# Softmax probability as a difference of two exponentials, with ScalarE's and TensorE's queues in another order

## The chip, the cores and the metric

The kernel runs on one core of a Trainium2 chip. A core has TensorE (PE, matmuls; its weight loads are shown as PEld), VectorE (DVE), ScalarE (ACT), GpSimd (POOL) and SyncE (SP, which here issues the DMAs). Each engine works through its own queue in order; they are tied together by semaphores. The metric is device time in microseconds of one execution, the lower the better.

## The reference, cut to what matters

`x` is 8 x 56 x 56 tokens of 64 channels, float32. Two layers follow each other, each a mixer and a mixture of experts:

```python
# layer 0 mixer: 49 regions (8x8 tokens) per image, 8 heads of 8 channels
idx_r = top_k(q_region @ k_region, 4)                  # 4 regions for every region
attn  = einsum('..sd,..kd->..sk', qs * scale, key_g)   # 64 queries x 256 keys, per head
score, index = top_k(attn, 32)                         # the 32 largest scores of a row
a_g   = softmax(score)                                 # over those 32
out   = a_g @ v_sel                                    # then a depthwise 3x3 conv of v is added,
out   = out @ out_w + out_b                            # and the output projection
# layer 0 experts: 8 experts 64->64->64, top 2 by a softmax router, exact GELU
# layer 1 mixer: 3x3 convolution 64->64 with weights binarized to +-1
# layer 1 experts: 8 experts 64->128->64, top 2, exact GELU
```

The kernel doesn't gather the 32 selected values. It makes a probability for all 256 keys that is zero for those not selected, and multiplies it with all 256 values.

## The kernel before, in words

The work is cut into 392 regions of 64 tokens for the attention, and into 56 strips of 7 regions (448 tokens) for everything else. Four stages run in one software pipeline: `a` (normalise, q, k, v), `t` (choose the 4 regions), `b` (attention, one region at a time) and `c0`, `c1` (what is done with a strip in layer 0 and in layer 1: the mixer's end, the router, the experts). Time is written in **slots**: one slot is one region of stage `b`, 14 slots are one **turn** (two strips), and `b` takes 28 turns. The table `PLACES` says in which slot, and at which fraction of it, an engine's queue holds a step of another stage; a step repeats every 7 slots. So slots are alike modulo 7, and the text calls them slot 0 to slot 6 by that remainder. ACT's slots with experts (GELU) are: slot 0 with two experts of `c1`, slots 2 and 3 with two of `c0` each, slots 5 and 6 with three of `c1` each. Slot 1 holds the end of layer 0's mixer (`c0` step 0: the depthwise convolution and the output projection in one group of matmuls into `h_ps`, read by ACT as `c_yT`), slot 4 that of layer 1. Stage `a` has its matmuls and copies at the end of slots 0 and 1.

One region in stage `b`, before:

- PE multiplies q and k (`pe_scores`, L425) into `s_ps`, ACT copies them to `b_s` (`act_scores`, L435). This is done two regions ahead.
- DVE selects (`dve_select`): four rounds over four tiles of 128 x 256 scores; `MAX8` (L452) takes the eight largest of each row into `b_v8`, `MATCH_REPLACE8` (L463) writes the scores to `b_r` with those eight replaced by `GONE` (-3e38).
- ACT (`act_sum`, L475 and L478) negates the row maximum (`b_nm`), takes the exponential of the 32 selected scores with their sum (`b_den`), and then (`act_exp`, L485) the exponential of all 256 (`b_e`).
- POOL takes the reciprocal of the sum (L493, `b_rec`), makes a mask times that reciprocal from `b_r` (`pool_mask`, L502), and multiplies it into `b_e` (`pool_prob`, L510).
- PE transposes `b_e` in two halves (`pe_turn`, L524) into the one bank `pT_ps`, ACT copies each half (`act_turn`, L532, `b_pT`), PE multiplies with the values (`pe_values`, L545, `o_ps`), and ACT copies the result to `b_at` (`act_values`, L552). PE and ACT do these for region r-1 in slot r.

`b_s`, `b_r`, `b_e` have two buffers, so the selection of region r+2 waits until the probability of region r is done (`b_prob`). An expert is a matmul (L666), GELU on ACT (L737, `c_h`), a matmul that spreads its weight (L669) and its copy on ACT (L739, `c_cb`), a product on POOL (L762) and a matmul down (L685). GELU and Exp are in different tables of ACT, so a switch puts an `ACT_TABLE_LOAD` in its queue.

## Time and profile before

| | |
|---|---|
| time, median of 3 runs | 6430.86 us (6424.47 to 6435.86) |
| time of the profiled execution | 6440.11 us |
| its span, first to last instruction | 6438.2 us |
| busy: DVE, PE, POOL, ACT | 87%, 74%, 69%, 63% of the span |
| mean granted TensorE clock | 0.73 of full speed |

Busy shares are averages over a start (stage `a` alone), 28 turns with stage `b`, and an end in which only `c0` and `c1` run. An engine's idle time is put down in the profile to what released it. All times here are in us unless ns is written.

### The profile page before, as it was taken

Reading aid. Unit: us, or ns where it says so; the run is one execution under the profiler, and the core shown is the slowest. Engines: PE = TensorE matmul, PEld = TensorE weight load, DVE = VectorE, ACT = ScalarE, POOL = GpSimd, SP = SyncE. Lnnn points to the kernel's source line nnn. Section 1 sums busy time; section 2 is a strip of 40 time slices with the busy share of each in tenths; the row PEclk is TensorE's granted clock in tenths of the full one; section 3 lists DMA queues with packets and bytes.
Section 4 is the critical chain, followed back from the end, with each engine's and each line's share of the span. In section 5 each row is a group of like instructions: output and inputs, shape, how many; then the busy total and the mean of one; then the engine's idle time right before and its main releaser. Section 6 shows DMA issues by size and latency. Waiting matters only on the chain.

```text
span 6438.2 us, 135940 instructions
## 1 busy us (share of the span) xinstructions
PE 4737.3 (74%) x26938; PEld 2880.6 (45%) x26938; DVE 5596.4 (87%) x24453; ACT 4054.4 (63%) x10222; POOL 4425.8 (69%) x3986
## 2 busy tenths in 40 slices
PE   3566777777777777777777777777777777777776
PEld 1333444444444444444444444444444444444444
DVE  1999999988989998999989898989999899999941
ACT  2455666666666666666666666666666666666643
POOL 1667776767677776767677677767776777777742
PEclk9666767777777777777777777777777777777777
DMA  4111111111111111111111111111111111111100
GB/s 75 39 31 42 34 40 34 40 32 42 30 41 34 39 35 34 40 32 43 32 42 30 40 36 36 38 33 40 32 43 31 43 31 32 30 30 34 33 11 10
DMA packets 585501, 229.09 MB, mean 36 GB/s; under 512 B 481152, under 2 KB 580224, under 8 KB 584576
## 3 DMA queue, kind: packets, MB, share of 16 engines
q1 hardware_dynamic: 584576, 219.25, 15.4%
q8 instruction: 276, 4.52, 0.3%
q14 instruction: 649, 5.32, 0.3%
HBM read 150.14 MB, written 68.80 MB: 34 GB/s over the span
## 4 chain that ended last, share of the span: by engine, by line
PE 29%; ACT 18%; issue 16%; DVE 15%; POOL 12%; ACTq 0%; DVEq 0%; POOLq 0%; DMA 0%; SPq 0%
DVE b_v L452 7%; POOL b_r L502 5%; PE y_ps L685 4%; DVE b_r L463 4%; PE h_ps L611 4%; POOL c_h L762 4%; ACT b_x L478 3%; PE a_ps L666 3%; PE pT_ps L524 3%; PE o_ps L545 2%; ACT b_e L485 2%; ACT L737 2%; PE h_ps L666 2%; POOL b_rec L493 2%; ACT L478 2%
## 5 line engine op out<-in xcount | busy, mean ns | idle before, releaser
L463 DVE MATCH_REPLACE8 b_r<-b_v,b_r 128x256 f32<-128x256 f32 x4704 | 1879.1, 416 | 0.0
L502 POOL TENSOR_SCALAR b_r<-b_r,b_rec 128x256 f32<-128x256 f32 x1568 | 1777.1, 1147 | 119.6 <-POOL b_rec L493 119.6
L452 DVE MAX8 b_v<-b_r 128x8 f32<-128x256 f32 x4704 | 1649.2, 418 | 0.0
L524 PE MATMUL pT_ps<-k_ident,b_e 128*128 128x128 f32 x3136 | 669.9, 352 | 776.3 <-ACT b_pT L532 688.3
L493 POOL TENSOR_TENSOR b_rec<-b_den,k_mone 128x4 f32<-128x4 f32 x392 | 400.5, 1022 | 1153.5 <-ACT b_x L478 1150.2
L762 POOL TENSOR_TENSOR c_h<-c_h,c_cb 128x448 f32<-128x448 f32 x672 | 760.9, 1133 | 503.9 <-ACT c_cb L739 503.0
L524 PEld LDWEIGHTS pT_ps<-k_ident,b_e 128*128 128x128 f32 x3136 | 472.6, 180 | 1161.2 <-issue 1136.2
L510 POOL TENSOR_TENSOR b_e<-b_e,b_r 128x1024 f32<-128x1024 f32 x392 | 923.5, 2356 | 18.0 <-POOL b_r L502 14.4
L685 PE MATMUL y_ps<-k_w,c_h 128*112 128x64 f32 x5376 | 776.1, 298 | 181.1 <-POOL c_h L762 177.9
L685 PEld LDWEIGHTS y_ps<-k_w,c_h 128*112 128x112 f32 x5376 | 706.5, 210 | 404.1 <-issue 403.0
L452 DVE MAX8 b_v<-b_s 128x8 f32<-128x256 f32 x1568 | 551.1, 415 | 318.0 <-POOL b_e L510 201.2
L532 ACT ACTIVATE b_pT<-pT_ps 128x512 f32<-128x512 f32 x784 | 469.9, 599 | 432.3 <-PE pT_ps L524 432.0
L485 ACT ACTIVATE b_e<-b_s,b_nm 128x256 f32<-128x256 f32 x1568 | 662.1, 493 | 0.0
L463 DVE MATCH_REPLACE8 b_r<-b_v,b_s 128x256 f32<-128x256 f32 x1568 | 624.7, 413 | 0.0
L666 PE MATMUL h_ps<-c_xT,k_w 128*128 128x448 f32 x672 | 525.4, 879 | 74.0 <-issue 67.5
L425 PE MATMUL s_ps<-b_k,b_q 32*128 32x256 f32 x3136 | 559.5, 484 | 24.2 <-DMA b_q<-q_d 24.2
L435 ACT ACTIVATE b_s<-s_ps 128x512 f32<-128x512 f32 x784 | 427.0, 603 | 117.5 <-PE s_ps L425 117.3
L478 ACT ACTIVATE b_x<-b_v,b_nm 128x32 f32<-128x32 f32 x1568 | 484.2, 310 | 9.5
L666 PE MATMUL a_ps<-c_xT,k_w 128*128 128x448 f32 x672 | 451.5, 765 | 0.0
L425 PEld LDWEIGHTS s_ps<-b_k,b_q 32*128 32x128 f32 x3136 | 336.3, 233 | 155.7 <-issue 119.6
L463 DVE MATCH_VALUE_LOAD b_r<-b_v,b_r 128x8 f32 x4704 | 405.3, 86 | 0.0
L737 ACT ACTIVATE c_h<-h_ps,k_b 128x448 f32<-128x448 f32 x336 | 212.8, 633 | 271.2 <-PE h_ps L666 268.5
(146 smaller groups left out, 7904.9 us busy)
## 6 DMA issues: line engine op xcount, KB each, us to landing
q_d<-a_qe SPq DMA_DIRECT2D x56, 448.0 KB, 4.2
b_k<-k_d SPq DMA_DIRECT2D x1568, 16.0 KB, 2.0
b_v<-v_d SPq DMA_DIRECT2D x1568, 16.0 KB, 2.0
b_q<-q_d SPq DMA_DIRECT2D x392, 64.0 KB, 2.1
c_win<-vpad_d SPq DMA_DIRECT2D x56, 145.0 KB, 2.8
c_hm<-cpad_d SPq DMA_DIRECT2D x56, 145.0 KB, 2.3
vpad_d<-a_vT SPq DMA_DIRECT2D x56, 116.0 KB, 3.7
c_win<-vpad_d SPq DMA_DIRECT2D x56, 116.0 KB, 2.7
```

The source lines that it names most:

```text
L425: last = pe.matmul(s_ps[g][:, t * NKEY:(t + 1) * NKEY], b_q[r % RING][part, 2 * t:2 * t + 2, :].rearrange("c h t -> c (h t)"), b_k[r % RIN ...
L452: top = dve.max(out=b_v8[p][:, t, 8 * rnd:8 * rnd + 8], in_=src[:, t, :])
L463: last = dve.match_replace(out=b_r[p][:, t, :], in_to_replace=b_v8[p][:, t, 8 * rnd:8 * rnd + 8], in_values=src[:, t, :], imm_value=GONE)
L478: last = act.activation(b_x8[:, t, :], b_v8[p][:, t, :], ACT.Exp, bias=b_nm[p][:, t:t + 1], accum_out=b_den[p][:, t:t + 1])
L485: last = act.activation(b_e[p][:, t, :], b_s[p][:, t, :], ACT.Exp, bias=b_nm[p][:, t:t + 1])
L493: pool.tensor_tensor(out=b_rec[p][:, :], in0=b_den[p][:, :], in1=k["mone"][:, 0:HP], op=ALU.pow).then_inc(b_inv, 1)
L502: last = pool.tensor_scalar(out=b_r[p][:, t, :], in0=b_r[p][:, t, :], scalar1=GONE, scalar2=b_rec[p][:, t:t + 1], op0=ALU.is_le, op1=ALU.mult)
L510: pool.tensor_tensor(out=b_e[p][:, :, :], in0=b_e[p][:, :, :], in1=b_r[p][:, :, :], op=ALU.mult).then_inc(b_prob, 1)
L524: last = pe.transpose(pT_ps[:, col:col + 128], b_e[p][:, t, c * 128:(c + 1) * 128], k["ident"][:, :])
L666: pe.matmul(bank[:, 0:STRIP], w1[layer][:, g, :], D["xT"][:, :], start=True, stop=True).then_inc(S["h"], 1)
L685: last = pe.matmul(y_ps[0:TILE, t * C:(t + 1) * C], D["h"][g % 2][:, t * TILE:(t + 1) * TILE], w2[layer][:, g, :], start=False, stop=(g == ...
L762: pool.tensor_tensor(out=D["h"][g % 2][:, :], in0=D["h"][g % 2][:, :], in1=D["cb"][g % 2][:, :], op=ALU.mult).then_inc(S["hc"], 1)
```

## The change

The probability is now `(exp(s) - exp(r)) / sum`, where `s` are the scores and `r` the scores with the 32 selected replaced by `GONE`, so that exp(r) is zero there and equal to exp(s) elsewhere.

- ACT takes a second exponential, in place on `b_r`, in two halves (`act_rest`), each as soon as DVE has finished two of the four tiles.
- POOL subtracts (`pool_prob`, two halves); `pool_mask` is gone. The reciprocal is no longer multiplied in here: PE spreads it over the partitions with four small matmuls into the free columns of `o_ps`, ACT's copy to `b_at` is 256 columns wide instead of 128, and POOL multiplies the two halves of `b_at` once a strip (`NORM`, before the projection).
- The row maximum is taken after the first round, and exp(s) of region r+1 stands at the end of ACT's slot r. ACT's slot begins with the copy of the transposed half.
- PE's slot begins with the transposes and the scores too; steps that stood ahead of them now stand behind.
- `PLACES`: `c0` step 0 goes from 78.1 to 78.62 on PE and from 78.3 to 78.64 on ACT. Layer 1's normalisation, transpose and gate (`c1` steps 1 to 3 on DVE, 2 and GATE on PE and ACT) move a slot ahead.

```diff
 def dve_select(dve, tau, r):
-            dve.wait_ge(b_prob, reg + 1)
+            dve.wait_ge(b_prob, 2 * reg + 2)
+            dve.wait_ge(b_sum, reg + 1)
...
+        def act_exp(act, tau, r):
+            act.wait_ge(b_max, reg + 1)
             act.activation(b_nm[p][:, :], b_v8[p][:, :, 0], ACT.Copy, scale=-1.0).then_inc(b_neg, 1)
...
+        def act_rest(act, tau, r):
+            for half in range(2):
+                act.wait_ge(b_sel, 2 * reg + half + 1)
+                for t in range(2 * half, 2 * half + 2):
+                    last = act.activation(b_r[p][:, t, :], b_r[p][:, t, :], ACT.Exp, bias=b_nm[p][:, t:t + 1])
+                last.then_inc(b_rest, 1)
...
+        def pool_prob(pool, tau, r):
+            for half in range(2):
...
+                pool.wait_ge(b_rest, 2 * reg + half + 1)
+                pool.tensor_tensor(out=b_e[p][:, pair, :], in0=b_e[p][:, pair, :], in1=b_r[p][:, pair, :],
+                                   op=ALU.subtract).then_inc(b_prob, 1)
...
-        def pool_mask(pool, tau, r):
...
 def pe_values(pe, tau, r):
+            pe.wait_ge(b_inv, reg + 1)
+            for t in range(HP):
+                pe.matmul(o_ps[32 * t:32 * t + VH, 128:256], b_rec[r % 2][:, t:t + 1].broadcast_to([128, VH]), k["ident"][:, :],
+                          start=True, stop=True)
...
 def act_values(act, tau, r):
-                           o_ps[:, 0:128].rearrange("c (j h q) -> c j h q", j=2, h=RH), ACT.Copy).then_inc(b_att, 1)
+                           o_ps[:, 0:256].rearrange("c (j h q) -> c j h q", j=4, h=RH), ACT.Copy).then_inc(b_att, 1)
...
 def pe_c(pe, tau, i, step, layer, other):
-                    pe.wait_ge(b_att, NWIN * (s + 1) + 1)
+                    pe.wait_ge(b_nrm, s + 1)
...
 def pool_c(pool, tau, i, step, layer):
+            if step == NORM:
+                pool.wait_ge(b_att, NWIN * (s + 1) + 1)
+                pool.tensor_tensor(out=b_at[i][:, 0:2], in0=b_at[i][:, 0:2], in1=b_at[i][:, 2:4], op=ALU.mult).then_inc(b_nrm, 1)
...
-                ("c0", 0): 78.1, ("c0", TURN): 78.5, ("c0", TURNED): 78.68, ("c0", 2): 81.66, ("c0", GATE): 82.05,
+                ("c0", 0): 78.62, ("c0", TURN): 78.7, ("c0", TURNED): 78.8, ("c0", 2): 81.66, ("c0", GATE): 82.05,
...
 @block.scalar, slot r
-                            act_sum(act, b, r)
-                            act_exp(act, b, r)
-                        steps(act, "act", n, lo, r, fs, 0, 0.2)
                             act_turn(act, b, r - 1, 0)
+                        if on:
+                            act_rest(act, b, r)
                             act_scores(act, b, r + 2)
                             act_turn(act, b, r - 1, 1)
-                        steps(act, "act", n, lo, r, fs, 0.2, 0.4)
-                        steps(act, "act", n, lo, r, fs, 0.4, 0.6)
+                        if on:
+                            act_sum(act, b, r)
+                        steps(act, "act", n, lo, r, fs, 0, 0.2)
                             act_values(act, b, r - 1)
-                        steps(act, "act", n, lo, r, fs, 0.6, 1)
+                        steps(act, "act", n, lo, r, fs, 0.2, 1)
+                        if on and (r + 1 < SLOTS or not last):
+                            act_exp(act, b, r + 1)
```

On ACT a slot with two experts (slot 0) stands like this before; names in brackets are the semaphores waited for.

```order
L475 ACTIVATE b_nm<-b_v 128x4 [waits b_top,b_prob]
L478 ACTIVATE b_x,b_den<-b_v,b_nm 128x32 [waits b_neg]
...
L485 ACTIVATE b_e<-b_s,b_nm 128x256 x4
L737 ACT_TABLE_LOAD [waits c1_h]
L737 ACTIVATE c_h<-h_ps,k_b_1 128x448 [waits c1_used]
L739 ACTIVATE c_cb<-g_ps 128x448 [waits c1_h]
L532 ACTIVATE b_pT<-pT_ps 128x512 [waits b_pt,b_pv]
L435 ACTIVATE b_s<-s_ps 128x512 [waits b_qk,b_exp]
...
L532 ACTIVATE b_pT<-pT_ps 128x512 [waits b_pt]
L737 ACTIVATE c_h<-a_ps,k_b_1 128x448 [waits c1_h,c1_used]
```

And the same slot after, from its first instruction to `b_at`, with the region's second exponential in it:

```order
L536 ACTIVATE b_pT<-pT_ps 128x512 [waits b_pt,b_pv]
...
L488 ACTIVATE b_r<-b_r,b_nm 128x256 [waits b_sel]
...
L435 ACTIVATE b_s<-s_ps 128x512 [waits b_qk,b_exp]
L435 ACTIVATE b_s<-s_ps 128x512
L536 ACTIVATE b_pT<-pT_ps 128x512 [waits b_pt]
L495 ACTIVATE b_x,b_den<-b_v,b_nm 128x32 x4
...
L747 ACTIVATE c_h<-h_ps,k_b_1 128x448 [waits c1_h]
...
L749 ACTIVATE c_cb<-g_ps 128x448 [waits c1_h]
...
L561 ACTIVATE b_at<-o_ps 128x32x8 [waits b_pv]
```

The copies of the transposed halves have moved to the head of the slot; the exponentials and the sum stand between them and the first GELU, and exp(s) of the next region closes the slot.

On PE the group of `c0` step 0 (L611 to L616, later L621 to L626) in slot 1, before:

```order
L611 MATMUL h_ps<-c_win,lepe_tap 64x448 [waits c0_x_in0]
L611 MATMUL h_ps<-c_win,lepe_tap 64x448 x2
L611 MATMUL h_ps<-c_row,lepe_tap 64x448
L612 MATMUL h_ps<-c_cor,lepe_tap 64x448
L616 MATMUL h_ps<-b_at,k_att 64x448 [waits b_att]
L616 MATMUL h_ps<-b_at,k_att 64x448
L524 MATMUL pT_ps<-k_ident,b_e 128x128 [waits b_prob,b_ptc]
L524 MATMUL pT_ps<-k_ident,b_e 128x128 x3
L425 MATMUL s_ps<-b_k,b_q 128x256 [waits b_in3,b_sc]
```

and after, from the last of the slot's value matmuls on:

```order
L554 MATMUL o_ps<-b_pT,b_v 16x128 x3
L702 MATMUL g_ps<-ident_b,c_x 128x112 [waits c0_part]
L702 MATMUL g_ps<-ident_b,c_x 128x112 x3
L709 MATMUL g_ps<-ident_b,c_x 64x112 [waits c1_lc,c0_pT]
L709 MATMUL g_ps<-ident_b,c_x 64x112 x3
L621 MATMUL h_ps<-c_win,lepe_tap 64x448 [waits c0_x_in1]
L621 MATMUL h_ps<-c_win,lepe_tap 64x448 x2
L621 MATMUL h_ps<-c_row,lepe_tap 64x448
L622 MATMUL h_ps<-c_cor,lepe_tap 64x448
L626 MATMUL h_ps<-b_at,k_att 64x448 [waits b_nrm]
L626 MATMUL h_ps<-b_at,k_att 64x448
L640 MATMUL a_ps<-k_ident,c_yT 112x64 [waits c0_pT,c0_yT]
```

The group stood ahead of the slot's transposes and scores; it now stands behind everything of stage `b` in that slot, directly ahead of the transposes (L640) of its own result.

On POOL a slot of `c0`'s experts, before and after:

```order
L493 TENSOR_TENSOR b_rec<-b_den,k_mone 128x4 [waits b_sum]
L502 TENSOR_SCALAR b_r<-b_r,b_rec 128x256 [waits b_inv,b_sel]
L502 TENSOR_SCALAR b_r<-b_r,b_rec 128x256 x3
L762 TENSOR_TENSOR c_h<-c_h,c_cb 128x448 [waits c0_cb] x2
L510 TENSOR_TENSOR b_e<-b_e,b_r 128x1024 [waits b_exp,b_msk]
```

```order
L508 TENSOR_TENSOR b_e<-b_e,b_r 128x512 [waits b_exp,b_rest]
L508 TENSOR_TENSOR b_e<-b_e,b_r 128x512 [waits b_rest]
L516 TENSOR_TENSOR b_rec<-b_den,k_mone 128x4 [waits b_sum]
L775 TENSOR_TENSOR c_h<-c_h,c_cb 128x448 [waits c0_cb] x2
```

The probability no longer stands behind the reciprocal, the four masks and the experts' products.

## Rows read from the trace of the kernel before

**Rows 1.** The page: busy time by engine.

```profile
PE 4737.3 (74%) x26938; PEld 2880.6 (45%) x26938; DVE 5596.4 (87%) x24453; ACT 4054.4 (63%) x10222; POOL 4425.8 (69%) x3986
```

**Rows 2.** Timeline of DVE: first selections of turns 3, 23 and 27.

```profile
723.05 1.08 DVE L452 MAX8 b_v<-b_s 128x8 f32<-128x256 f32 x3 [0.22 <-issue]
5154.06 1.08 DVE L452 MAX8 b_v<-b_s 128x8 f32<-128x256 f32 x3
5965.81 1.41 DVE L452 MAX8 b_v<-b_s 128x8 f32<-128x256 f32 x4
```

**Rows 3.** Windows (busy of PE, PEld, DVE, ACT, POOL; clock; DMA): nine turns, late, end.

```profile
2719.70:4713.40 1993.70, 1503.21 (x8658) 915.70 (x8658) 1804.52 (x7848) 1313.11 (x3295) 1421.64 (x1280) 0.73 0.16 37
...
5000.00:6000.00 1000.00, 761.72 (x4517) 472.76 (x4517) 956.07 (x4187) 680.11 (x1724) 757.14 (x669) 0.75 0.14 33
6164.00:6438.20 274.20, 199.09 (x933) 120.68 (x931) 46.16 (x275) 97.23 (x174) 87.61 (x95) 0.74 0.05 12
```

**Rows 4.** DVE's waits in the nine turns: total, times, longest.

```profile
DVE b_v L452 <- POOL b_e L510: 89.9, 18, 5.8
DVE b_v L452 <- issue: 34.2, 27, 3.2
```

**Rows 5.** Timelines of POOL and DVE around one such wait.

```profile
2993.59 1.03 POOL L493 TENSOR_TENSOR b_rec<-b_den,k_mone 128x4 f32<-128x4 f32 x1 [11.16 <-ACT b_x L478]
2994.92 4.51 POOL L502 TENSOR_SCALAR b_r<-b_r,b_rec 128x256 f32<-128x256 f32 x4 [0.30 <-POOL b_rec L493]
3001.95 2.35 POOL L510 TENSOR_TENSOR b_e<-b_e,b_r 128x1024 f32<-128x1024 f32 x1
...
3004.43 1.41 DVE L452 MAX8 b_v<-b_s 128x8 f32<-128x256 f32 x4 [4.84 <-POOL b_e L510]
```

**Rows 6.** ACT's waits in the nine turns.

```profile
ACT b_pT L532 <- PE pT_ps L524: 140.2, 93, 5.3
ACT b_at L552 <- PE o_ps L545: 101.2, 108, 3.0
ACT b_nm L475 <- DVE b_v L452: 89.9, 18, 5.7
ACT c_h L737 <- PE h_ps L666: 84.1, 41, 3.5
ACT c_h L737 <- PE a_ps L666: 72.9, 64, 2.3
ACT b_s L435 <- PE s_ps L425: 35.5, 65, 1.4
ACT a_vT L351 <- PE a_ps L327: 32.7, 18, 1.9
ACT a_xT L337 <- PE a_ps L257: 28.3, 18, 2.1
```

**Rows 7.** Two groups of ACT in the nine turns.

```profile
L739 ACT ACTIVATE c_cb<-g_ps 128x448 f32<-128x448 f32 x216 | 116.2, 538 | 0.0
...
L552 ACT ACTIVATE b_at<-o_ps 128x128 f32<-128x128 f32 x126 | 34.9, 277 | 101.2 <-PE o_ps L545 101.2
```

**Rows 8.** Timelines of ACT and PE in slot 1.

```profile
2973.77 1.69 ACT L485 ACTIVATE b_e<-b_s,b_nm 128x256 f32<-128x256 f32 x4
2980.53 0.60 ACT L532 ACTIVATE b_pT<-pT_ps 128x512 f32<-128x512 f32 x1 [5.06 <-PE pT_ps L524]
...
2971.52 4.71 PE L611 MATMUL h_ps<-c_win,lepe_tap 128*64 128x448 f32 x6 [3.12 <-ACT a_qe L344]
2978.18 1.72 PE L616 MATMUL h_ps<-b_at,k_att 128*64 128x448 f32 x4
```

**Rows 9.** Timelines: one expert matmul of 448 columns after work and after a wait; ACT's third GELU.

```profile
3002.98 0.97 PE L666 MATMUL h_ps<-c_xT,k_w 128*128 128x448 f32 x2
3010.81 1.70 PE L666 MATMUL a_ps<-c_xT,k_w 128*128 128x448 f32 x2
...
3046.69 0.63 ACT L737 ACTIVATE c_h<-h_ps,k_b 128x448 f32<-128x448 f32 x1 [3.53 <-PE h_ps L666]
```

100 lines of the change are left out of this document (42 added, 58 removed).

## The prediction

> **What bounds the kernel now.** I read the page first. DVE is busy for 87% of the span, PE for 74%, ACT for 63% [rows 1], so DVE looks like the bound, but the averages hide two things: the end has no stage `b`, and ACT's idle time is not free. So I read DVE's timeline for the starts of the turns. Turns 3 to 22 take from 723.05 to 5154.06, which is 4431.0 for 20 turns, or 221.5 a turn; turns 23 to 26 take 811.8, or 202.9 a turn [rows 2]. The 20 turns are 69% of the span, and the forecast is made there.
>
> Nine of them fill the window 2719.7 to 4713.4, 1993.7 long [rows 3]. In it DVE is busy for 1804.5, which is 200.5 a turn. Its waits for stage `b` are of two kinds [rows 4]: 89.9 for POOL's probability, twice a turn, 10.0 a turn, and 34.2 (3.8 a turn) called issue, mostly at the turn's branch. The rest of its idle time, some 7 a turn, is many small gaps. A turn in which DVE never waited for another engine's stage `b` work would take 221.5 - 10.0 = 211.5.
>
> Why is the probability late, when POOL is busy for only 1421.6 of 1993.7? The timeline of one such wait shows it [rows 5]. POOL had been idle for 11.16 until ACT's sum came; then it took reciprocal, mask (4.51), two products of experts and the probability (2.35), and DVE started 4.84 late. So what is late is ACT. Its table of waits says the same from the other side [rows 6]: ACT waits for DVE only 18 times in 126 slots, 10.0 a turn. In the other slots it is behind DVE, although it is busy for only 1313.1 (145.9 a turn). It has 680.6 of idle time, 75.6 a turn, and most is waiting for PE: 140.2 for the transposed halves, 101.2 for the value matmuls, 84.1 + 72.9 for the experts' first matmul, 35.5 for the scores. ACT and PE hand work to and fro, and this chain, with its waits, takes 221.5 - 10.0 = 211.5 a turn. DVE and ACT are thus two chains of equal length (211.5 each by this count), and each stalls the other once in 7 slots. A gain must come from both, and a loss on either shows at once.
>
> **The change, part by part, a turn of 14 slots.**
>
> *POOL* loses four masks a slot, 4.51 together [rows 5], and gains nothing of that size: the two subtractions have the 1024 columns of the old product (2.35), and `NORM` has 896 columns, so about 2.1, twice a turn. The cost is nothing, since POOL is not the chain. The probability of region r is ready about 2.6 after ACT's second exponential (one half of it overlaps), where it came 10.7 after the sum (2993.59 to 3004.30). In [rows 5] DVE started 10.8 after ACT's sum of two regions before (2993.59 to 3004.43); now it may start some 3 after ACT's second exponential. So the direct stall goes, as long as ACT keeps up.
>
> *ACT, added.* The second exponential is four ACTIVATEs of the kind that now takes 1.69 for four [rows 8]: 14 x 1.69 = 23.7. The wider copy of `o_ps`: 448 columns take 538 ns and 128 take 277 ns [rows 7], so 0.8 ns a column, 0.1 a slot, 1.5 a turn. Table loads: exp, GELU and back again in the same slots, and the router's Exp now stands beside the sum; counted in the order of the queues there are as many as before, so zero.
>
> *ACT, waits that go* (per turn, rows 6 divided by 9). The copy of the transposed half now follows a stretch in which ACT is taking exp(s) and PE has its transposes free: 15.6, all of it. The scores: 3.9, all. The value matmuls: PE does them while ACT takes the sum and changes its table, so the wait of 11.2 goes in the slots with experts; in slots 1 and 4 PE has the gate or layer 1's convolution ahead of the values, and I leave 0.5 and 2.2 (an estimate; the longest such wait is 3.0), twice each: 5.4 stay, 5.8 go. The experts: 17.4 now. The second GELU no longer waits, since `b_at` and the sum cover PE. The third must still wait for the first expert's product on POOL and its matmul down, 3.53 in the row of [rows 9]; I leave 3.5 in slot 5 and 2.0 in slot 6, twice: 11.0 stay, 6.4 go. Together 31.7 go.
>
> *ACT, waits that come.* The depthwise convolution and projection of layer 0 take PE from 2971.52 to 2979.90, 8.4 [rows 8]. Before, PE did them in the shadow of ACT's exponentials, and ACT still waited 5.06 for the transposes behind them (this is within the 15.6 above). Now they stand behind the value matmuls, and ACT has nothing but one copy (0.54) before it must read their result. What that wait costs hangs on the speed of PE in those 14 matmuls of 448 columns. They took 4.71 for six at first, just after PE had been idle for 3.12, and 1.72 for four at the end; a pair of such matmuls is 0.97 in a busy stretch and 1.70 after a wait of 3.55 [rows 8, 9], which is the clock's two levels, 2.4 and 1.2 GHz. The bounds are 14 x 0.45 - 0.5 = 5.8 and 14 x 0.85 - 0.5 = 11.4. As observed it would be 7.9. PE now comes to them out of other work rather than out of a wait, so I take 6.5, twice a turn: 13.0. The Trainium skill ("TensorE: Matmul & The Clock Gate", "What's actually happening") says that the throttled clock is the default and that activity releases it; the two durations of the row agree. By that rule alone the lower bound of 5.8 would hold, 1.4 a turn less.
>
> Smaller new waits: in slots 1 the transposes of that result, the split copies and the weights' transposes follow each other with nothing between them (2.3, an estimate), and in slots 0 layer 1's moved transpose stands behind the last expert's matmul down (3.3, an estimate from the 3.53 of the third GELU, which waits for such a matmul too [rows 9], and from which 1.3 of the later wait of `a_xT` comes off). Twice each is 8.6; I take 7.5, since ACT's handovers in slot 4 get shorter.
>
> *PE* gets four matmuls of 128 columns a slot, about 0.4, which lie under ACT's sum: zero; without that cover 5 a turn. Layer 1's gate a slot ahead moves work of DVE from one slot to the next; DVE's waits for it are not among the large ones [rows 4], so zero, with the 7 a turn of small gaps as the most that it could touch.
>
> **The sum.** ACT's chain: 211.5 + 23.7 + 1.5 - 31.7 + 13.0 + 7.5 = 225.5 a turn. DVE's own stays at 211.5 or a little less, so ACT sets the turn and DVE waits for it. That is +4.0 a turn, +80 over the 20. In turns 23 to 26 DVE is the bound (956 of 1000 busy [rows 3]) and ACT has slack. Without stage `a` ACT's busy time is 0.68 x 202.9 = 138.0, 7.9 less than in the others, and at least the waits for `a_vT` and `a_xT` are gone, 6.8 [rows 6]; the new chain would be 210.8, less what else of `a` falls away, so I take 208: +5 each, +20. Turns 0 to 2 have no layer 1 and are DVE's: zero. The end (274 [rows 3]) keeps its chain: zero, give or take 10. Total +100. The profiled execution took 6440.1, 0.14% above the median of the runs shown, 6430.9; on the median the sum gives 6531, and I say 6530.
>
> **The rivals.** *A: the handovers overlap better than I count, and it gets faster.* For it: 31.7 of going waits is an estimate from an order, PE's idle time in the window is 490 of 1994, and every wait that shrinks lets PE keep the full clock, which shortens the others. Against it: 25.2 a turn of new ACT work is certain. With every transpose, score and value wait gone, half of the experts' waits, 5.8 for the convolution and 3 for the small ones, the chain is 211.5 + 25.2 - 30.7 - 8.7 + 11.6 + 3.0 = 211.9, and DVE's 211.5 stands beside it; -9.6 a turn, -190: 6240 is its far end. With half of that gain, 216.5 a turn, it is 6330. It decides when ACT's idle time falls under 50.4 a turn (221.5 - 145.9 - 25.2); it is 75.6 now.
>
> *B: no change.* The added work and the waits removed cancel, ACT's idle time lands on that 50.4: 6420 to 6443.
>
> *C: the new wait is at its worst.* The 14 matmuls at the lower clock (11.4 instead of 6.5, +9.8 a turn) or waits for the values in all slots: 235.3 a turn, +276, with the later turns 6730 as its far end; with half of it, 230.4 a turn, 6630. Against it: PE is a little busier than before.
>
> *D: the change does not do what it says*: DVE still waits for its stage `b` inputs, because ACT is as late as before. This is part of my forecast and not against it: the wait moves from the mask to the second exponential.
>
> **How the numbers follow.** Forecast (6530, from 6455 to 6600): 0.45. A: 0.35. B: 0.08. C: 0.12. The range takes in A to its middle and past it, down to 6300, and the lower part of C, up to 6610; some 0.1 is left out on each side. This kernel's runs tell a difference of 0.2% (13) from none. Faster: A, 0.35. Same: B, 0.08. Slower: forecast and C, 0.57.
>
> **What would show it.** Right: in the nine-turn stretch a turn of 224 to 228; ACT busy near 171 a turn; the waits of `b_pT` and `b_s` near zero; a wait of ACT for `c_yT` from `h_ps` of 6 to 8, twice a turn, the largest; ACT's waits for DVE gone; DVE's stage `b` wait at 14 or more a turn, put down to the probability or to `b_sum`; POOL busy under 110 a turn. Wrong: ACT's idle time under 50 a turn, or ACT waiting for DVE again (then DVE is the bound and rival A holds); or the third GELU and the values waiting as much as before (rival C). The step I trust least is the size of the convolution's wait, then the 31.7.

## The result, and the profile after

The changed kernel takes 6616.6 us (median of 4 runs, 6612.3 to 6623.7) where the kernel before took 6433.4 on the same chip (6424.5 to 6449.5): the ratio is 1.0283, with a 95% interval of 1.0260 to 1.0306. It is slower, as forecast, but by 183 instead of 100: 16.6 above the forecast's own band (6455 to 6600) and 6.6 above the widest bound that the prediction gives (6610).

The page of the changed kernel, busy time by engine:

```profile
PE 4968.4 (75%) x30074; PEld 2973.9 (45%) x30074; DVE 5664.3 (86%) x24453; ACT 4622.6 (70%) x11790; POOL 2824.5 (43%) x2866
```

Beside [rows 1], POOL has 1601 less of busy time, and ACT works 568 more. DVE's share hardly moved, which by itself would say that nothing changed. So the starts of turns 3, 23 and 27 are read next, in the timeline of DVE:

```profile
719.62 0.75 DVE L453 MAX8 b_v<-b_s 128x8 f32<-128x256 f32 x2 [0.32 <-issue]
...
5291.20 0.76 DVE L453 MAX8 b_v<-b_s 128x8 f32<-128x256 f32 x2 [0.21 <-issue]
...
6135.31 0.43 DVE L453 MAX8 b_v<-b_s 128x8 f32<-128x256 f32 x1
```

Against [rows 2] the start took 3.4 less. Turns 3 to 22 took 4571.6 instead of 4431.0: 228.6 a turn, +7.0 each, +140.6 together. Turns 23 to 26 took 844.1 instead of 811.8, 211.0 a turn, +32.4. What comes after them took 475.2 instead of 472.4, by the two spans (6610.5 and 6438.2). The sum is +172, the difference of the spans; the loss is in the turns. Nine of them, the stretch 5000 to 6000 and the end, in windows with the columns of [rows 3] (5000 to 6000 is late turns for the most part: turn 23 starts at 5291.20 here and at 5154.06 before):

```profile
2779.10:4835.60 2056.50, 1572.30 (x9651) 940.77 (x9646) 1819.44 (x7848) 1493.31 (x3796) 905.83 (x919) 0.75 0.16 36
5000.00:6000.00 1000.00, 785.98 (x4856) 476.95 (x4854) 923.79 (x3971) 745.75 (x1912) 450.96 (x446) 0.75 0.14 33
6340.00:6610.00 270.00, 196.06 (x939) 119.89 (x938) 46.92 (x269) 96.42 (x176) 84.56 (x92) 0.74 0.05 12
```

A turn is 228.5. ACT is busy for 165.9 of it and idle for 62.6. ACT's waits in that stretch (total, times, longest) show where:

```profile
ACT c_yT L722 <- PE h_ps L626: 124.9, 18, 7.4
ACT t_a L381 <- PE a_ps L372: 65.0, 18, 3.7
ACT c_xT L731 <- PE g_ps L257: 57.7, 18, 4.1
ACT b_at L561 <- PE o_ps L554: 57.5, 18, 3.5
ACT b_pT L536 <- PE pT_ps L528: 41.9, 25, 5.1
ACT c_h L747 <- PE a_ps L676: 40.8, 21, 3.6
ACT c_h L747 <- PE h_ps L676: 37.9, 20, 2.6
ACT a_vT L351 <- PE a_ps L327: 34.3, 18, 1.9
ACT a_qk L342 <- PE a_ps L317: 31.7, 18, 2.1
```

Beside [rows 6], the 89.9 of waiting for DVE and the 35.5 for the scores are gone, `b_pT` and the experts' `c_h` have shrunk, and three rows that were small or absent stand on top: `c_yT`, `t_a`, `c_xT`. ACT never waits for DVE in turns 3 to 26. DVE waits for ACT:

```profile
DVE b_v L453 <- ACT b_x L495: 126.1, 18, 8.2
DVE b_v L453 <- issue: 28.3, 26, 3.7
```

That is 14.0 a turn, where [rows 4] had 10.0 for POOL. The largest of ACT's waits in the timelines of ACT and PE, in slot 1:

```profile
3050.75 0.38 ACT L561 ACTIVATE b_at<-o_ps 128x256 f32<-128x256 f32 x1
...
3052.61 0.54 ACT L756 ACTIVATE c_lop<-g_ps 64x448 bf16<-64x448 f32 x1 [0.73 <-PE g_ps L709]
3060.58 0.63 ACT L722 ACTIVATE c_yT<-h_ps,out_bias 64x448 f32<-64x448 f32 x1 [7.43 <-PE h_ps L626]
...
3052.36 4.70 PE L621 MATMUL h_ps<-c_win,lepe_tap 128*64 128x448 f32 x6
3056.85 1.15 PE L621 MATMUL h_ps<-c_row,lepe_tap 128*64 128x448 f32 x2
3057.93 0.96 PE L622 MATMUL h_ps<-c_cor,lepe_tap 64*64 64x448 f32 x2
3058.82 1.72 PE L626 MATMUL h_ps<-b_at,k_att 128*64 128x448 f32 x4
```

The 14 matmuls take 8.2, where they took 8.4 in [rows 8], but now ACT has no work beside them: it ends a copy at 3053.15 and stands until 3060.58. The first six still take 4.70, at the lower clock level: the granted clock is 0.50 in the windows from 3043.50 to 3057.00 and 0.96 from there to 3060.50.

### The profile page after: what moved, and what is told of

The parts are those of the page before. It is cut to its first block and busy times, and to the rows that moved or that the text cites. A ratio compares the mean times of both kernels' runs of the same rounds, so it can differ in the third digit from the quotient of the medians.

```text
span 6610.5 us, 144443 instructions
## 1 busy us (share of the span) xinstructions
PE 4968.4 (75%) x30074; PEld 2973.9 (45%) x30074; DVE 5664.3 (86%) x24453; ACT 4622.6 (70%) x11790; POOL 2824.5 (43%) x2866
## 5 line engine op out<-in xcount | busy, mean ns | idle before, releaser
L508 POOL TENSOR_TENSOR b_e<-b_e,b_r 128x512 f32<-128x512 f32 x784 | 982.5, 1274 | 2464.9 <-ACT b_r L488 2464.9
L528 PE MATMUL pT_ps<-k_ident,b_e 128*128 128x128 f32 x3136 | 727.3, 376 | 442.8 <-ACT a_qe L344 156.9
L695 PEld LDWEIGHTS y_ps<-k_w,c_h 128*112 128x112 f32 x5376 | 735.7, 217 | 450.9 <-issue 439.9
L488 ACT ACTIVATE b_r<-b_r,b_nm 128x256 f32<-128x256 f32 x1568 | 664.1, 496 | 86.7 <-DVE b_r L464 86.6
L425 PE MATMUL s_ps<-b_k,b_q 32*128 32x256 f32 x3136 | 688.1, 578 | 24.2 <-DMA b_q<-q_d 24.2
L554 PE MATMUL o_ps<-b_pT,b_v 128*16 128x128 f32 x6272 | 411.4, 325 | 134.0 <-ACT b_pT L536 133.9
L679 PE MATMUL g_ps<-c_cwT,sel_b 128*128 128x448 bf16 x672 | 281.5, 419 | 295.5 <-ACT c_cb L749 294.9
L464 DVE MATCH_VALUE_LOAD b_r<-b_v,b_r 128x8 f32 x4704 | 480.1, 102 | 0.0
L425 PEld LDWEIGHTS s_ps<-b_k,b_q 32*128 32x128 f32 x3136 | 395.7, 272 | 181.5 <-issue 130.3
L676 PE MATMUL h_ps<-c_xT,k_w 128*128 128x448 f32 x672 | 426.3, 725 | 5.2 <-ACT c_cwT L741 5.2
```

Of the source, the lines that this page charges most:

```text
L425: last = pe.matmul(s_ps[g][:, t * NKEY:(t + 1) * NKEY], b_q[r % RING][part, 2 * t:2 * t + 2, :].rearrange("c h t -> c (h t)"), b_k[r % RIN ...
L464: last = dve.match_replace(out=b_r[p][:, t, :], in_to_replace=b_v8[p][:, t, 8 * rnd:8 * rnd + 8], in_values=src[:, t, :], imm_value=GONE)
L488: last = act.activation(b_r[p][:, t, :], b_r[p][:, t, :], ACT.Exp, bias=b_nm[p][:, t:t + 1])
L508: pool.tensor_tensor(out=b_e[p][:, pair, :], in0=b_e[p][:, pair, :], in1=b_r[p][:, pair, :], op=ALU.subtract).then_inc(b_prob, 1)
L528: last = pe.transpose(pT_ps[:, col:col + 128], b_e[p][:, t, c * 128:(c + 1) * 128], k["ident"][:, :])
L695: last = pe.matmul(y_ps[0:TILE, t * C:(t + 1) * C], D["h"][g % 2][:, t * TILE:(t + 1) * TILE], w2[layer][:, g, :], start=False, stop=(g == ...
```

## The experiments

"Before" and "after" are the two kernels. The experiments were timed in 3 rounds beside the kernel before, whose medians were 6432.7 to 6438.8. e1, e3, e10 and e15 leave work out that the result needs and stand here for their time alone.

| run | us | ratio to before, 95% interval |
|---|---|---|
| after | 6616.6 | 1.0283 (1.0260 to 1.0306) |
| e1_no_second_exp | 6419.1 | 0.9973 (0.9962 to 0.9985) |
| e2_before_plus_exp | 7047.7 | 1.0952 (1.0934 to 1.0970) |
| e3_before_no_mask | 6449.9 | 1.0024 (1.0015 to 1.0034) |
| e4_sum_early | 6614.4 | 1.0282 (1.0265 to 1.0299) |
| e5_gate_back | 6584.6 | 1.0227 (1.0209 to 1.0244) |
| e6_conv_ahead | 6483.9 | 1.0071 (1.0049 to 1.0093) |
| e7_t_early | 6616.7 | 1.0279 (1.0262 to 1.0296) |
| e8_split_conv | 6503.1 | 1.0114 (1.0087 to 1.0140) |
| e9_before_exp_same_table | 6731.0 | 1.0461 (1.0444 to 1.0479) |
| e10_no_spread | 6658.8 | 1.0342 (1.0325 to 1.0360) |
| e11_all_places | 6251.9 | 0.9706 (0.9688 to 0.9724) |
| e12_before_pool_order | 6375.7 | 0.9902 (0.9885 to 0.9918) |
| e13_norm_early | 6630.1 | 1.0294 (1.0277 to 1.0312) |
| e14_all_but_split | 6436.4 | 0.9995 (0.9983 to 1.0007) |
| e15_places_no_exp | 6217.3 | 0.9652 (0.9635 to 0.9668) |
| e16_spread_twice | 6620.3 | 1.0280 (1.0263 to 1.0298) |

**The second exponential, in the new order and in the old.** Taken out of the changed kernel. POOL then adds `b_e` to itself and waits for DVE's selection, so its wait for ACT goes too:

```diff
 def act_rest
-                    last = act.activation(b_r[p][:, t, :], b_r[p][:, t, :], ACT.Exp, bias=b_nm[p][:, t:t + 1])
+            act.wait_ge(b_sel, 2 * reg + 2)
 def pool_prob
-                pool.tensor_tensor(... in0=b_e, in1=b_r, op=ALU.subtract)
+                pool.tensor_tensor(... in0=b_e, in1=b_e, op=ALU.add)
```

> The changed kernel without its second exponential on ACT (left out: exp(r); POOL adds b_e to itself with the same waits on the selection instead of subtracting). Theory (ACT's chain with PE sets the turn of 228.6 us): 14 x 1.6 us of ACT work fall away, the chain would be 206 a turn, which is under DVE's own 211 to 214, so DVE sets the turn and ACT waits for DVE again; 20 turns x -15 and some in the later turns: about 6290 us. Rival (the loss is DVE's new wait for the sum, 7 us twice a turn): the sum comes only 1.6 earlier, twice a turn: about 6550 us.

It gave 197 back, a time between the two. The window of nine turns, with the columns of [rows 3]:

```profile
2700.10:4692.00 1991.90, 1564.10 (x9640) 934.18 (x9639) 1792.99 (x7848) 1312.36 (x3287) 850.58 (x918) 0.74 0.16 37
```

and some of ACT's waits in it:

```profile
ACT c_yT L719 <- PE h_ps L623: 134.6, 18, 7.7
ACT b_at L558 <- PE o_ps L551: 90.5, 53, 4.7
ACT b_s L435 <- PE s_ps L425: 77.4, 98, 1.5
```

ACT has 20.1 a turn less to do (1493.3 against 1312.4, by nine), but the turn falls by only 7.2, to 221.3. The rest turns into waiting for PE: the scores' wait, zero in the changed kernel, is 77.4, and the values' rises. So the new order without its new work is only 0.3% faster than the old kernel, although ACT never waits for DVE in these nine turns. Two attempts at the reverse, an exponential of the same size in the old order, on a constant tile, with a result that nobody uses:

```diff
+        def act_extra(act, tau, r):
+            for t in range(HP):
+                act.activation(b_x9[:, t, :].rearrange("p (a b) -> p a b", a=2), k["w1_1"][:, 0:2, :], ACT.Exp, bias=b_nm[p][:, t:t + 1])
...
                             act_turn(act, b, r - 1, 0)
+                        if on:
+                            act_extra(act, b, r)
```

> The kernel before, with four more exponentials of 128x256 on ACT in every slot (of a constant tile, result not used), between the copy of the first transposed half and the scores. Theory: before, ACT's chain is 211.5 of 221.5 us a turn, so 14 x 1.6 = 22.4 more make 234 a turn, +12.4, 20 turns +250, later turns +30: about 6710 us; the changed kernel at 6617 has then got about 90 us back by its order and by the mask taken off POOL. Rival (before, DVE is the bound and ACT's idle time, 25% of the turn, takes the work in): 6430 to 6480 us.

7047.7, far outside both: this one measured something else. Between two GELUs an Exp needs its table and then GELU's again: ACT had 12310 instructions instead of 10222, 1568 of them the added Exp and the other 520 table loads of 1.28 us. In e9 the same four lines stand right behind `act_exp`, in the same table:

> The kernel before with four more exponentials of 128x256 on ACT in every slot, as in the earlier run of this kind, but directly behind exp(s), where the Exp table is loaded; the earlier place added 520 table loads (667 us busy) beside the 1568 ACTIVATEs, so its 7048 us measured both. Theory: ACT's chain of 211.5 us a turn gets 14 x 1.6 = 22.4 more, less what now lies in waits for PE that follow (the 5.06 us wait behind the convolution, twice a turn, takes 3.2 of it in): 231 a turn, 20 turns +190, later turns +30: about 6650 us. Rival 1 (ACT's waits take nothing in): 6710. Rival 2 (as in the new order, where leaving the second exponential out gave back only 7.3 of 22.4 a turn): +7 a turn, 6590 us.

+298, above the theory and both rivals: the added work costs 1.5 times as much in the old order as taking it out of the new one gives back (197; the two edits are not exact mirrors, since e1 also frees POOL of a wait). And from this kernel to the changed one it is 114 down (6731 to 6617), which is what all the rest of the change together gives back. e2 is 317 slower than e9: that is what the 520 added table loads cost, about 0.6 each.

**POOL's mask.** In the kernel before, without the mask:

```diff
 def pool_mask
-            for t in range(HP):
-                last = pool.tensor_scalar(out=b_r[p][:, t, :], in0=b_r[p][:, t, :], scalar1=GONE, scalar2=b_rec[p][:, t:t + 1], ...)
 def pool_prob
-                               in0=b_e[p][:, :, :], in1=b_r[p][:, :, :], op=ALU.mult
+                               in0=b_e[p][:, :, :], in1=b_e[p][:, :, :], op=ALU.mult
```

> The kernel before without POOL's four masks a slot (left out: the mask; the product is b_e with itself, all waits kept). Theory (two chains of 211.5 us, each stalling the other, joined by POOL's lateness): DVE's 10.0 a turn of waiting for the probability go, the turn becomes 212 to 214, 20 turns x -8.5: about 6260 us. Rival (ACT with PE alone sets the turn, POOL's lateness is only a symptom): 6410 to 6430 us.

No gain: it is 0.2% slower, above both expectations. DVE's wait in 2000 us is as long as in [rows 4]:

```profile
DVE b_v L452 <- POOL b_e L505: 93.1, 18, 5.6
```

and the timeline of POOL in a slot with experts shows why:

```profile
2944.70 1.01 POOL L493 TENSOR_TENSOR b_rec<-b_den,k_mone 128x4 f32<-128x4 f32 x1 [1.52 <-ACT b_x L478]
2948.88 1.14 POOL L757 TENSOR_TENSOR c_h<-c_h,c_cb 128x448 f32<-128x448 f32 x1 [3.17 <-ACT c_cb L734]
2954.65 1.13 POOL L757 TENSOR_TENSOR c_h<-c_h,c_cb 128x448 f32<-128x448 f32 x1 [4.64 <-ACT c_cb L734]
2955.75 1.89 POOL L505 TENSOR_TENSOR b_e<-b_e 128x1024 f32<-128x1024 f32 x1
```

The probability stands behind the experts' two products in POOL's queue, and these wait for ACT's copies. In the kernel before, in the very place of [rows 5], the second product still waited for its copy when the mask was done:

```profile
2999.40 1.13 POOL L762 TENSOR_TENSOR c_h<-c_h,c_cb 128x448 f32<-128x448 f32 x1
3000.86 1.13 POOL L762 TENSOR_TENSOR c_h<-c_h,c_cb 128x448 f32<-128x448 f32 x1 [0.33 <-ACT c_cb L739]
```

So the 4.51 of the mask lay in that wait, and the order of POOL's queue is part of the stall of [rows 4]. e12 tries that on the kernel before, with the two products and their matmuls down behind the probability in slots 2 and 9:

```diff
+                late = slot == 86
-                PLACES["pe"][f"c{layer}", DOWN + g] = slot + down
+                PLACES["pe"][f"c{layer}", DOWN + g] = slot + (0.65 + g / 100 if late else down)
-                PLACES["pool"][f"c{layer}", UP + g] = slot + pool_up
+                PLACES["pool"][f"c{layer}", UP + g] = slot + (0.55 + g / 100 if late else pool_up)
```

> The kernel before with POOL's queue changed in slots 2 and 9 alone: the probability stands ahead of the two experts' products instead of behind them (their products at 0.55 and 0.56, their matmuls down on PE at 0.65 and 0.66). The run without the mask showed that DVE's wait of 5 us stays when the mask is gone. Theory (what is late is the second expert's copy on ACT, ahead of the probability in POOL's queue): DVE's wait falls from 5.0 to 2, 20 turns x -6: about 6320 us. Rival (ACT's chain takes over at once, since the ends of both are tied to each other): 6400 to 6440 us.

It gained 1.0%, or 57 us, between theory and rival, where a stall of 10 a turn would be 200 over 20 turns. DVE's wait for POOL's probability is 49.3 in 2000 us, where [rows 4] had 89.9; it was halved, not removed, and DVE now waits 53.7 for the router's `c_p`, where it waited 19.7 in the nine turns before.

**DVE's wait for the sum.** In the changed kernel ACT's sum is put ahead of the scores' copy and the second half of the transposes:

```diff
                             act_rest(act, b, r)
+                            act_sum(act, b, r)
...
-                            act_sum(act, b, r)
```

> The changed kernel with ACT's sum directly behind the second exponential, ahead of the scores and the second copy. Theory: DVE's wait for the sum is a symptom, so the time stays within 0.4% of the changed kernel, 6595 to 6640 us. Rival (that wait is the loss): the sum comes 1.5 us earlier in each of the two stalls of a turn, 20 x -3: about 6555 us.

No change. DVE's largest wait keeps its size (130.4 in 2000 us) and changes its name, to ACT's copy of the scores (`b_s`). So the sum's place is not the loss: DVE waits for whatever ACT does last there.

**The places.** Each of these moves steps in the changed kernel's table. First layer 1's router back to where it was (normalisation, transpose and gate a slot later, and ACT's exponential for it at 108.68 instead of 108.05, which puts it behind the experts of its slot again):

```diff
-                 ("c1", 1): 103.66, ("c1", 2): 105.66, ("c1", 3): 107.66
+                 ("c1", 1): 104.66, ("c1", 2): 106.66, ("c1", 3): 108.66
...
-                ("c1", 0): 102.1, ("c1", TURN): 102.5, ("c1", TURNED): 102.68, ("c1", 2): 105.695, ("c1", GATE): 106.05,
+                ("c1", 0): 102.1, ("c1", TURN): 102.5, ("c1", TURNED): 102.68, ("c1", 2): 106.695, ("c1", GATE): 107.05,
...
```

> The changed kernel with layer 1's normalisation, transpose and gate back in their old slots (c1 steps 1 to 3 and GATE, one slot later). Theory (the turn is the chain of ACT and PE): ACT's wait for c_xT in slots 0 and 7 (6.4 us a turn) goes, and one for it behind layer 0's weights in slots 1 and 8 comes (0.4 each before, with GATE's matmuls moved to slots 2 and 9 under ACT's sum): 20 turns x -5, about 6520 us. Rival (the gate's move is neutral, the wait is filled by another): 6600 to 6630 us.

32 back, between theory and rival; the prediction had set this cost to zero. In 2000 us `c_xT` is gone from ACT's waits and `t_a` is halved, from 65.0 to 32.6, but 50.4 for `a_xT` came, and DVE waits 125.5 for the router's logits (`c_lm` from `c_lg`) instead of for the sum. Then the convolution and projection where they had been (the transposes of the experts' weights, `c0` step 4, go back with them, from 85.85 to 85.64):

```diff
-                ("c0", 0): 78.62, ("c0", TURN): 78.7, ("c0", TURNED): 78.8,
+                ("c0", 0): 78.1, ("c0", TURN): 78.5, ("c0", TURNED): 78.68,
-                 ("c0", 0): 78.64, ("c0", TURN): 78.72,
+                 ("c0", 0): 78.3, ("c0", TURN): 78.52,
```

> The changed kernel with c0 step 0 back at 78.1 on PE (ahead of the value matmuls, behind the transposes) and 78.3 on ACT, its transposes and the weights' at their old places. Theory: ACT's wait for c_yT (6.9 us) becomes a wait for the value matmuls of nearly the same size, less what the sum covers (1.2 twice a turn), so 6570 to 6620 us. Rival (the place behind the values is what costs): 14 us a turn go, about 6340 us.

133 back, more than the theory's 0 to 47 and less than the rival's 277. ACT's wait for `c_yT` left the list, and most of it came back in front of the values, which now stand behind the convolution in PE's queue:

```profile
ACT b_at L561 <- PE o_ps L554: 175.0, 36, 7.8
```

The second name in the list, `t_a`, was moved ahead by itself, on PE and (59.8 to 59.3) on ACT:

```diff
-            pe={("a", 3): 7.9, ("a", 4): 8.9, ("t", 1): 59.8,
+            pe={("a", 3): 7.9, ("a", 4): 8.9, ("t", 1): 59.28,
```

> The changed kernel with the t stage's matmul and its copy at 59.28 and 59.3 instead of 59.8, ahead of the second expert. Theory: ACT's wait for t_a (3.6 us, twice a turn, not foreseen) becomes 0.5, 20 turns x -6: about 6500 us. Rival (the wait only moves to the next thing PE does late, as the run without the second exponential showed for others): 6590 to 6620 us.

Nothing, as the rival said. Its wait was gone; in its place stood a wait of 84.3 of ACT for the experts and one of 75.9 of DVE for POOL's `c_rs`. A row of waits is thus no price.

Last the convolution was cut in two. The matmuls of its taps (five in the kernel's text, ten records in the trace) don't need the attention, and go to the end of slot 0, behind stage `a`'s matmuls (77.93), where PE waited for ACT's `a_qe`; the projection stays late:

```diff
-            if step == 0:
+            if step == LEPE or (step == 0 and layer == 1):
...
+            if step == 0:
+                if layer == 0:
                     pe.wait_ge(b_nrm, s + 1)
-            pe={("a", 3): 7.9, ("a", 4): 8.9,
+            pe={("a", 3): 7.9, ("a", EVICTED): 7.97, ("c0", LEPE): 77.93, ("a", 4): 8.9,
```

> The changed kernel with the five convolution matmuls of c0 step 0 moved to the end of slots 0 and 7 on PE, behind the last matmul of stage a and ahead of PE's wait for its copies, so that they run under ACT's copies of q and k, its table load and exp(s); only the two projection matmuls stay behind the values. Theory: of 6.9 us of waiting for c_yT about 2 stay, and about 1.5 come at the first transposes of slots 1 and 8: 2 x -3.5 a turn, 20 turns: about 6470 us. Rival (PE itself is the bound, its order doesn't matter): 6600 to 6630 us.

113 back, somewhat less than expected.

**All places together.** Gate back, taps split off, projection at 78.1, and `NORM` from 78.2 to 77.6:

> The changed kernel with the places that the runs favour put together: layer 1's gate in its old slot, the convolution matmuls split off to the end of slots 0 and 7 on PE, the projection back ahead of the values, and POOL's NORM at 77.6, a slot earlier, since in the split kernel PE still waited 4.5 us for it behind POOL's reciprocal. Theory (each place is a wait of ACT for PE, 1.6, 5.7 and 6 us a turn): about 6390 us, below the kernel before. Rival (the gains overlap): 6450 to 6490 us.

6251.9 (four runs, 6233.3 to 6287.5; the trace is of the slowest): this kernel beats both, the old by 2.9%, and by far more than either theory allowed. By the starts of turns 3 and 23 a turn is 213.7. Three runs take it apart. With `NORM` alone moved:

```diff
-            pool={("a", 1): 4.9, ("c0", NORM): 78.2,
+            pool={("a", 1): 4.9, ("c0", NORM): 77.6,
```

> Leaves nothing out. The changed kernel with one place moved: POOL's normalisation of the attention (b_at times b_at) from 78.2 to 77.6, so that it is issued a slot earlier on POOL. If the convolution is late only because it is issued behind the values, the taps that run ahead of its wait for the normalisation still cover POOL, and the time stays within 6595 to 6630 us. If the normalisation is what holds the projection (POOL has it behind the probability of slot 1, which waits for ACT's second exponential), the wait of ACT for c_yT falls from 7 us to under 4 and the time comes to 6550 to 6580.

Nothing. With all except the split (the edits of e5, e6 and e13):

> Leaves nothing out. The kernel of all places without the split of the convolution: gate back, the whole convolution at 78.1 and its copy at 78.3, normalisation at 77.6. Gate and convolution alone measured 32 and 133 us of gain, whose sum gives 6617 - 165 = 6452 us. If the split carries the rest of the 365 us that all places gave, this run stays near 6452 (6430 to 6480). If the early normalisation does, because at 78.2 it makes the early projection wait for POOL behind the second exponential, this run comes near 6300 (6260 to 6340).

6436.4, near the plain sum of 6452, and the same as the kernel before: with the old places back, the exponential and the new order cost nothing on balance. The split on top of this gives the other 184, more than the 113 that it gave by itself. Part of the difference may be `NORM`: with the split alone (e8) PE still waited 33.4 in 2000 us for it (`h_ps` from POOL's `b_at`, 1.9 each; the 4.5 that e11's expectation gives is ACT's wait for `c_yT`), a wait that e11 doesn't have, and no run has all places without the earlier `NORM`. Nor was the split tried in the kernel before, so the 2.9% are of the change and the split together. The timeline of PE around the transposes that open slot 1, without the split (e14):

```profile
3062.68 1.08 PE L528 MATMUL pT_ps<-k_ident,b_e 128*128 128x128 f32 x4 [3.37 <-ACT a_qe L344]
3063.69 2.08 PE L425 MATMUL s_ps<-b_k,b_q 32*128 32x256 f32 x8
3065.79 1.09 PE L528 MATMUL pT_ps<-k_ident,b_e 128*128 128x128 f32 x4
3066.81 3.85 PE L621 MATMUL h_ps<-c_win,lepe_tap 128*64 128x448 f32 x6
```

and with it (e11):

```profile
3208.89 3.25 PE L623 MATMUL h_ps<-c_win,lepe_tap 128*64 128x448 f32 x6
3211.98 0.91 PE L623 MATMUL h_ps<-c_row,lepe_tap 128*64 128x448 f32 x2
3212.82 0.96 PE L624 MATMUL h_ps<-c_cor,lepe_tap 64*64 64x448 f32 x2
3213.72 0.66 PE L530 MATMUL pT_ps<-k_ident,b_e 128*128 128x128 f32 x4
3214.30 1.13 PE L427 MATMUL s_ps<-b_k,b_q 32*128 32x256 f32 x8
```

In e14 PE stands idle for 3.37, and then does the transposes, the scores and the transposes again at the lower level: 1.08, 2.08, 1.09, at a granted clock of 0.50 from 3062.60 to 3066.80. In e11 it fills that wait with the taps and comes to the same work at the full clock: 0.66, 1.13, at 1.00 from 3211.90 to 3215.50. So it is in all 18 such places of the stretch 2700 to 4700: the scores take 2.08 on average in e14 and 1.13 in e11. The taps, 5 us long, no longer stand between transposes and values. In 2000 us ACT's wait for the values is 78.8 in e11 and 158.0 in e14. And the exponential once more, out of the kernel of all places (the edit of e1):

> Leaves out the second exponential (the probability is then the sum of the first with itself), in the kernel of all places. If exponential and places are two separate losses, it gains again what it gained in the changed kernel, 197 us: 6055 us. If the order has made ACT's chain shorter than DVE's work (DVE is 94% busy in the turns there), the gain is small, 40 to 120 us: 6130 to 6210, with DVE above 95% busy.

Only 35, a little under the smallest gain of 40 that the second theory named. With the spread of e11's four runs and the two intervals it can be anything from some 20 to 50. The windows 2700 to 4700 of e11 and of e15, with the columns of [rows 3]:

```profile
2700.00:4700.00 2000.00, 1598.76 (x10031) 961.83 (x10028) 1886.03 (x8164) 1553.38 (x3946) 953.52 (x961) 0.77 0.17 38
```

```profile
2700.00:4700.00 2000.00, 1591.37 (x10210) 948.42 (x10209) 1905.77 (x8278) 1388.68 (x3479) 905.69 (x969) 0.78 0.17 38
```

DVE is busy for 94% in the one and 95% in the other. With ACT relieved of 20 a turn and the time hardly lower, DVE is the bound here, and the exponential that cost 298 in the old order and 197 in the changed one costs 35 under it.

**The spread matmuls.** Taken out of the changed kernel, and done twice:

```diff
 e10, in pe_values
-            for t in range(HP):
-                pe.matmul(o_ps[32 * t:32 * t + VH, 128:256], b_rec..., k["ident"][:, :], start=True, stop=True)
 e16
-            for t in range(HP):
+            for t in 2 * list(range(HP)):
```

> The changed kernel without PE's four small matmuls a slot that spread the reciprocal (left out; their columns of the bank stay zero). The prediction priced them at nothing, 5 us a turn without cover. Theory (ACT and PE alternate, ACT has the sum and a table load while PE does these): only slots 1, 4, 8 and 11 show them, 20 turns x -1.5: 6575 to 6615 us. Rival (PE is the bound): 20 x -5: about 6510 us.

> Does the four spread matmuls of each window twice (the second time with the same operands into the same place), else the changed kernel. If leaving them out cost 42 us because TensorE's granted clock fell (0.748 to 0.715), doubling them holds or raises the clock (0.75 to 0.77) and the time is between 6580 and 6620 us although some 0.3 us of matmuls a window are added to the chain. If the clock follows something else, the added matmuls show as a loss: 14 windows by 0.3 to 0.6 us is 4 to 8 us a turn, 6700 to 6800 us at an unchanged clock.

Less work made it 42 slower, outside both expectations; twice the work made no difference. The mean granted clock of the profiled executions is 0.715 without, 0.748 with, 0.758 with them doubled. (Each of the four matmuls of the kernel's text is two records in the trace.) The windows 2800 to 4800 of after, of e10 and of e16, a fence each:

```profile
2800.00:4800.00 2000.00, 1529.36 (x9400) 912.47 (x9399) 1768.95 (x7632) 1453.10 (x3693) 879.60 (x890) 0.75 0.16 35
```

```profile
2800.00:4800.00 2000.00, 1548.26 (x8328) 924.25 (x8329) 1767.60 (x7593) 1439.96 (x3653) 874.15 (x885) 0.71 0.16 35
```

```profile
2800.00:4800.00 2000.00, 1547.78 (x10359) 945.19 (x10358) 1796.26 (x7620) 1454.56 (x3686) 880.20 (x891) 0.76 0.16 35
```

PE's group of the experts' first matmul in the same stretch (busy, mean ns), of after and then of e10:

```profile
L676 PE MATMUL h_ps<-c_xT,k_w 128*128 128x448 f32 x209 | 128.3, 703 | 0.0
```

```profile
L673 PE MATMUL h_ps<-c_xT,k_w 128*128 128x448 f32 x206 | 138.4, 765 | 0.0
```

e10 has 1072 matmuls fewer in the same 2000 us and PE is busy for longer, because the others stretch: 703 to 765 ns here, and 299 to 317 for the matmul down. That the clock made e10 slow fits all of this, but no run changed the clock alone, and the mean clock alone doesn't set the time (e4 has 0.756 at the time of the changed kernel's 0.748). So it stays the likeliest cause and not a shown one.

## Why the prediction was right or wrong

*The bound.* Right that ACT and PE together set the turn in the changed kernel: DVE's own part is 228.5 - 14.0 = 214.5, moving what DVE waits for changed nothing (e4), and moving PE's and ACT's steps gave 32, 133 and 113 (e5, e6, e8). e15 shows the limit from the other side. That the old kernel had two chains of equal length was not borne out as it was meant: without the mask (e3) DVE's stall stayed, and with half of it gone (e12) the gain was 57 and not 100.

*POOL.* "The cost is nothing" was right (100.6 a turn, under the 110). But the reading of [rows 5] stopped one step early. The products of the experts stood between mask and probability and waited for ACT's copies; the mask cost nothing (e3). This did no harm to the sum, since what was forecast to go, DVE's direct wait, went either way.

*ACT, added.* The second exponential is 23.7 a turn, as summed (213.0 in nine turns). The wider copy is 1.5 (385 ns in place of 277). Yet ACT's busy time rose by only 20.0. Instructions of ACT that follow each other without a wait overlap by about 0.1 each, and in the changed kernel more of them do: neighbours overlap by 35.2 a turn, where it was 25.2, and 4.2 of the new 10.0 were already in the 1.69 for four. The sum forgot the rest, and was 5.2 a turn too high.

*ACT, waits that go.* 28.4 of the forecast 31.7. The scores went fully. `b_pT` kept 4.7 where zero was said, of which 3.8 is one wait a turn (3.2 to 5.1), at the turn's branch. The values keep 6.4 (5.4 said), the experts 8.7 (11.0 said).

*ACT, the wait that comes.* `c_yT` is 13.9 a turn, where 13.0 was said: the largest, twice a turn, of 6.9. This was the step trusted least, and its size held, but its reason did not: PE does come to the matmuls out of other work, from 3043.54 to 3052.36 with gaps of no more than 0.82, and still did all of that and the first six taps at the lower level (4.70 for the six, 4.71 in the old row). The Trainium skill ("TensorE: Matmul & The Clock Gate", "What's actually happening") says that the throttled clock is the default and activity releases it; by that rule alone the wait would have been the prediction's lower bound of 5.8, and the 6.9 measured lies between it and the 7.9 of the old row.

*The step that failed: "Smaller new waits: ... I take 7.5".* The rows that grew come to 12.5 a turn: 7.2 for `t_a`, which the prediction doesn't name at all, 5.1 more for `c_xT` (57.7 in the nine turns, 11.6 before), 3.1 for `c_cwT`, `c_lop` and `c_hmp` together (30.2, before 2.0), and 2.9 less for `a_xT` (2.2, before 28.3). One wait for `t_a` in the timelines of ACT and PE:

```profile
3088.26 0.56 ACT L749 ACTIVATE c_cb<-g_ps 128x448 f32<-128x448 f32 x1
3092.50 0.20 ACT L381 ACTIVATE t_a<-a_ps 7x49 f32<-7x49 f32 x1 [3.67 <-PE a_ps L372]
...
3088.99 3.22 PE L695 MATMUL y_ps<-k_w,c_h 128*112 128x64 f32 x16 [0.90 <-POOL c_h L775]
3092.14 0.33 PE L372 MATMUL a_ps<-t_k,t_q 64*7 64x49 f32 x2
```

The matmul of `t_a` stands behind the experts' last matmuls down, just as the prediction said of layer 1's transpose, and ACT has nothing left to do beside them. Before, the copy to `b_at` and the router's exponential with a table load of 1.28 lay in between (in the timeline of the kernel before, 3015.04 to 3016.86). Moving the router away was one cause: with it back, the wait is halved (e5). The whole by the same steps:

| a turn | said | measured |
|---|---|---|
| ACT's chain before | 211.5 | 211.5 |
| work added (busy time) | +25.2 | +20.0 |
| waits that go | -31.7 | -28.4 |
| `c_yT` | +13.0 | +13.9 |
| other waits (measured: the remainder) | +7.5 | +11.5 |
| turn | 225.5 | 228.5 |

So the failing terms are the small waits, 4.0 too hopeful, and the waits that go, 3.3 too hopeful; the overlap took 5.2 the other way, so that a sum of three misses came out only 3.0 off. This is a book of where the time lies and not a list of causes: e7 took the wait for `t_a` away by itself and the time didn't move. Three more a turn is 60.6 over the 20 turns. The late turns were said to be 208 each and are 211.0, which is 12.4 more. There the forecast looked at ACT alone, but DVE's own busy time rose as well, from 781.1 of 811.8 to 795.8 of 844.1, while it waited only 7.8 for ACT's sum; how the 12.4 divides was not tested. Together that is 73 of the 83 by which +183 differs from +100. The other ten are the difference between profiled executions and medians: by the two spans the loss is 172.

*"Layer 1's gate a slot ahead: zero."* Wrong by 32 (e5), at most 1.6 a turn, within the 7 that it was said to touch. *The spread matmuls: "zero; without that cover 5 a turn".* Adding four more did cost nothing (e16), but taking them away made the kernel 42 slower (e10), which no term of the sum allowed for.

*What the sum could not see.* It took the order as given. e9, e1 and e15 say that the same work costs about 298, 197 or 35, by the order around it. The loss of 183 is the exponential together with an order that puts the convolution, the projection and the router where ACT has nothing else to do. It goes when either is taken back: 6419.1 without the exponential (e1), 6436.4 with the old places (e14). With the taps split off as well it is 2.9% faster than before.

*The signals.* Right: `c_yT` on top at 6 to 8, the scores' wait zero, ACT's waits for DVE gone, DVE's wait at 14.0 behind ACT's sum, POOL under 110. Wrong: a turn of 228.5 where 224 to 228 was said, ACT's busy time of 165.9 (near 171 was said), and `b_pT`, which is not near zero.

*Rivals.* A (the hand-overs overlap better, faster) needed ACT's idle time under 50.4 a turn; it is 62.6. e11 gets there by other places: 446.6 idle in 2000, or 47.7 of a turn of 213.7. B fell. The time, 228.5 a turn, came nearer to the middle of C (230.4) than to the forecast, but not by what C names: the values wait for less than before, and `c_yT` is 6.9 and not 11.4.

## What to carry to other kernels

When two engines hand work to and fro, price a reordering by where the second one stands idle in the new order, and put the waiting engine's independent work (here the ten taps) into that idle time rather than between two hand-overs; that was worth 113 us here by itself and 184 on top of the other places, as much as the whole change cost. The length of a wait in a table is no price: taking away DVE's for the sum and ACT's for `t_a` changed nothing, while moving the work behind `c_yT` gave 133. When an added operation comes out expensive, test it in the new order and in the old before giving it up, since its price was about 298, 197 and 35 us in three orders.
